# Attention stage: the eight gathers of a group's expert rows issued in one run, behind the LayerNorm root and the bias addition

## The reference, cut to what matters

```python
x = x + L0_xattn(layernorm(x), ctx, ctx)      # mLSTM cell, 8 heads
x = x + L0_ffn(layernorm(x))                  # mixture of 8 experts, top 2, and one shared expert
x = x + L1_xattn(layernorm(x), ctx, ctx)      # softmax attention, 16 heads
x = x + L1_ffn(layernorm(x))                  # 8 experts by position
```

```python
q = split(layernorm(x) @ Wq.T + bq);  k = split(ctx @ Wk.T + bk);  v = split(ctx @ Wv.T + bv)
x = x + softmax(q k^T * SCALE) v @ Wp.T + bp
```

## Time and profile before

| | us |
|---|---|
| median of 3 timed runs (1168.09 to 1171.35) | 1169.76 |
| the profiled execution, whole | 1156.03 |
| its span in the trace | 1154.0 |

### The profile page before, as it was taken

The page is one execution under the profiler, slowest core; times in us unless marked ns, Lnnn a source line. Parts: engine busy times, 40 slices in busy tenths (PEclk is TensorE's granted clock), DMA queues, the critical chain, the costliest instruction groups (busy, mean ns, idle before and its releaser), DMA issues. The chain is left out here.

```text
span 1154.0 us, 24802 instructions
## 1 busy us (share of the span) xinstructions
PE 957.6 (83%) x9121; PEld 684.5 (59%) x9121; DVE 734.0 (64%) x2271; ACT 534.4 (46%) x848; POOL 507.2 (44%) x566
## 2 busy tenths in 40 slices
PE   6819998665777766999997279899899899989998
PEld 1217776444555543666665157777777778856665
DVE  7776999765566652878776455555566656345553
ACT  2457886422333322676665234445455455323231
POOL 4302675676566660555554765434544521011110
PEclk9959998886778767999999569988989989989999
DMA  8554553321222234233332211111111310024331
GB/s 258 196 156 137 160 164 108 122 95 51 60 60 67 63 99 126 96 126 120 120 125 80 62 36 39 39 29 29 47 38 32 88 43 20 21 69 109 95 92 36
DMA packets 84598, 101.28 MB, mean 88 GB/s; under 512 B 36128, under 2 KB 57312, under 8 KB 83712
## 3 DMA queue, kind: packets, MB, share of 16 engines
q1 hardware_dynamic: 56576, 78.20, 22.2%
q0 software_dynamic: 8192, 16.79, 5.0%
q10 hardware_dynamic: 19712, 4.72, 2.5%
HBM read 64.81 MB, written 30.67 MB: 83 GB/s over the span
## 5 line engine op out<-in xcount | busy, mean ns | idle before, releaser
L1701 ACT ACTIVATE split_table<-attn_psT 128x1024 f32<-128x1024 f32 x64 | 65.5, 1024 | 163.9 <-DMA early_ctxT<-in_ctxT 94.1
L1022 POOL TENSOR_TENSOR moe_h_lo<-moe_hid,moe_h_hi 128x512 f16<-128x512 f32 x78 | 90.6, 1163 | 103.3 <-ACT moe_h_hi L1175 98.4
L1169 ACT ACTIVATE moe_act_g<-moe_psG,split_unscale 128x512 f32<-128x512 f32 x110 | 75.5, 687 | 66.5 <-PE moe_psU L1104 32.4
L1279 DVE SCALAR_TENSOR_TENSOR moe_hid<-moe_psU,split_to_hidden,moe_act_g 128x512 f32<-128x512 f32 x110 | 81.0, 748 | 37.8 <-ACT moe_act_g L1169 37.7
L1592 PE MATMUL attn_psO<-heads_vheads,split_table 128*64 128x18 f32 x2048 | 81.8, 214 | 24.9 <-issue 24.8
L1592 PEld LDWEIGHTS attn_psO<-heads_vheads,split_table 128*64 128x64 f32 x2048 | 72.7, 140 | 37.0 <-issue 35.7
L1764 DVE TENSOR_REDUCE split_table<-attn_psN 128x16 f32<-128x1024 f32 x62 | 75.7, 1221 | 17.0 <-PE attn_psN L1555 9.0
L1175 ACT ACTIVATE moe_h_hi<-moe_hid 128x512 f16<-128x512 f32 x110 | 68.4, 622 | 35.0 <-DVE moe_hid L1279 17.6
L1016 POOL DMA_INDIRECT scratch_xs<-cell_xn,res_row x64 | 63.1, 986 | 41.5 <-DVE res_row L1273 24.3
L1788 DVE RECIPROCAL split_table<-attn_psO 128x16 f32<-128x16 f32 x64 | 16.5, 257 | 101.8 <-PE attn_psO L1592 66.1
L1016 POOL DMA_INDIRECT scratch_xs<-moe_xn,res_row x64 | 63.2, 987 | 38.3 <-DVE res_row L1273 20.8
(11 more groups left out here) (282 smaller groups left out, 2788.7 us busy)
## 6 DMA issues: line engine op xcount, KB each, us to landing
early_ctxT<-in_keys SPq DMA_DIRECT2D x16, 512.0 KB, 3.6
scratch_ys<-cell_h SPq DMA_DIRECT2D x26, 256.0 KB, 2.0
early_ctxT<-in_values SPq DMA_DIRECT2D x8, 544.0 KB, 3.7
mlstm_vals<-in_values SPq DMA_DIRECT2D x8, 544.0 KB, 4.0
res_x<-in_x SPq DMA_DIRECT2D x16, 256.0 KB, 6.2
early_ctxT<-in_ctxT SPq DMA_DIRECT2D x16, 256.0 KB, 6.3
attn_in_ctxT<-attn_in_ctxT ACTq DMA_DIRECT2D x64, 64.0 KB
scratch_x<-split_table SPq DMA_DIRECT2D x16, 256.0 KB
```

The source lines that it names most:

```text
L1022: pool.tensor_tensor(h_lo[u % 3][c][:, :], hid[u % 2][c][:, :], h_hi[u % 3][c][:, :], ALU.subtract).then_inc(lo_done[c], 1)
L1169: act.activation(act_g[c][:, :], psG[c][:, :], ACT.Silu, scale=sw.unscale[:, 0:1]).then_inc(silu_done, 1)
L1279: v.scalar_tensor_tensor(out=hid[u % 2][c][:, :], in0=psU[c][:, :], scalar=sw.to_hidden[:, 0:1], in1=act_g[c][:, :], op0=ALU.mult, op1=ALU ...
L1701: act.activation(probT[i % 2][:, :, :, :, :].rearrange("p r b m q -> p (r b m q)"), psT[:, :], ACT.Exp).then_inc(prob_done, 1)
```

## The change

```diff
             add_bias(0)
             add_bias(1)
             for g in range(GROUPS - 2):
-                if there(g + 4):
-                    gather(g + 4, (0, 1))
                 if there(g + 3):
                     ln.root(pool, g + 3, (g + 3) % 2)
+                add_bias(g + 2)
                 if there(g + 4):
-                    gather(g + 4, (2, 3))
-                add_bias(g + 2)
+                    gather(g + 4)
             ffn.ln.power_const(pool)
             ffn.ln.root(pool, 0, 0)
```

## The result

The change makes the kernel slower: median 1221.32 us (1217.76 to 1221.72, 6 runs) against 1169.18 (1155.19 to 1173.89, 6 runs) in the same comparison, a ratio of 1.0489 with a 95% interval of 1.0440 to 1.0537. I had said 1171, and 1158 to 1183. The profiled execution took 1220.95 us, against 1156.03 before. In after, lines from 1527 on are two lower than in the kernel before (values are L1590, combine is L1741); the kernels of the experiments shift them further by what their edits add. The one trace of before is of an execution 13.1 us under its median, the one of after of an execution at its median, so of the 64.9 us between their spans the medians bear out 52.1.

A forecast was written before the change was run, and what follows sets the result against it. It took TensorE to bound the passes, with GpSimd mattering through what it makes others wait for. All terms were 0 except +0.90 us in the last pass, giving 1156.9 profiled, 1171 with 13.7 added for the median; range 1158 to 1183.

The forecast's parts named there:

- GpSimd's own times: In a steady pass, counted from S (the root's start): bias at 1.35, first transfer at 2.84, eighth at 11.73 us.
- Root and bias: On GpSimd in each pass: root still waits for statistics, bias moves 5.1 us ahead with nobody delayed; 0 each.
- The case that the prediction priced at 1.1 us: In a pass, split_peak's second half on VectorE waits for the early bias; covered by VectorE's idle time, so 0.
- Transfers and the new loop: Root, bias, eight transfers, landing, combine, statistics, root: at most 20.42 us, under 20.71; 0 in the ten middle passes.
- the new loop binds: Rival, chance 0.12: transfers in a run of eight land 1 us later, so combine delays passes; 1175 us.
- Last pass: The last pass with gathers, 19.81 us before, takes as long as the pass of 20.71: +0.90 us.
- TensorE in the ten middle passes: Between first and last pass: as many transfers in the same 11 us, so 0; ends -13.6 and +16.5 us.
- The first pass: Loses four transfers ahead of its root, keeps eight behind, taken as one run already before: 0, ends 0 and -1.8 us.
- a longer run holds TensorE up more: Rival, chance 0.20: TensorE's backlog gets no pause, its clock drops more often; about 1187 us, 1179 with half the passes.
- One interruption less: Rival, chance 0.28: TensorE is held up at a run's start, not by each transfer; 1.10 us less a pass, about 1160.

The follow-up runs named there:

- e2: Changed kernel with the bias put behind the unbroken run of eight transfers: 1215.06 us, ratio 1.0423 to the kernel before.
- h1: Changed kernel with an addition of 0.83 us on GpSimd behind each of the first three pairs of transfers: 1161.32 us, ratio 1.0092 to before.
- e4: Changed kernel with transfers issued two at a time, the bias or a wait for ScalarE's exponentials between: 1102.10 us, ratio 0.9435 to before.
- g1: Changed kernel with each indirect transfer fetching 32 rows and not 128, still in runs of eight: 1233.23 us, ratio 1.0573 to before.
- e1: Changed kernel with the bias moved between two runs of four transfers, all behind the root: 1173.53 us, ratio 1.0044 to before.
- e3: Changed kernel without the 96 transfers of groups 4 to 15, whose combines take old rows without waiting: 1095.59 us, ratio 0.9373 to before.
- f2: Changed kernel with the same bytes fetched by SyncE as plain transfers of consecutive rows, in runs of eight: 1095.00 us, ratio 0.9356 to before.
- f5: Changed kernel with GpSimd issuing the 96 transfers as plain ones of consecutive rows, in runs of eight: 1094.88 us, ratio 0.9355 to before.

## Why the prediction was wrong

*GpSimd's own times* were right to 0.01 us: bias at S + 1.35, first transfer at S + 2.84, last one at S + 11.74 (S + 11.73 was said).

*Root and bias* at 0 were right: the root still waits for the statistics (idle for 14.6 us ahead of it), and e2 shows that the bias's place is worth little. The case that the prediction priced at 1.1 us, split_peak behind a bias that came first, did not arise: its second half starts at S + 1.31 (882.26), 0.04 us ahead of the bias, and takes 0.23 us beside 0.22 before.

*Transfers and the new loop* did not bind, as forecast: in after combine comes 4.2 us behind the earliest point that the loop allowed (S + 18.46 against S + 14.26). Its price was sound, though: h1 has 2.51 us of landing where 2.53 was taken. The rival "the new loop binds" (0.12) is false for after, and true for h1.

*Last pass*: +0.90 said; it took 27.96 us (990.32 to 1018.28) where 19.81 had been, +8.2. It was priced at a pass with two runs of four, while it is one with a run of eight.

*TensorE in the ten middle passes* is the step that failed. It took 0, with ends of -13.6 and +16.5; the ten cost 51.0 (718.68 to 990.32 is 271.64, less 220.67). The first pass, at 0 too, adds 5.5 (26.53 less 21.03) and the last 8.2: 64.6 in all, rounding aside. Three things were wrong in it:
- "In the same 11 us as many transfers are made, beside the same values" took the cost to go by the number of transfers. It goes by how many stand in a row: e4 makes the same eight for 0.3 us, g1 fetches a quarter of the rows for 11.
- The upper end came from the longest pass that the trace had, 23.72. But every pass of before had runs of four, so none of them bounds a run of eight. The first pass was even read as "one run of eight, as in effect before"; two runs of four with 1.4 us between are not that, as e1 shows (1.0044 against 1.0489).
- The waits of TensorE were taken as the size of the hold. Gaps on "issue" grow from 23.7 to 27.5 us while 48 us are lost, and in e2 they are 42.9 us for nearly the same loss. How late a result was taken up follows the run better: at most 0.68 us for values with no transfers (e3), 1.51 with four, and now 7.1 with eight. It has to be looked for at every consumer, though: in e2 it is the exponential that is 7.7 us late.

The rival *a longer run holds TensorE up more* (0.20) named the mechanism, and the clock with it, and what I put against it ("the total of transfers is unchanged") was the false step. Its price of 1187 at most was too small by 34 us. *One interruption less* (0.28) has the sign wrong: the hold does not come at a run's start, since pairs cost almost nothing.

The Trainium skill says in "SBUF — State Buffer", "SBUF: two separate sides", that DMA and the compute engines can't slow each other. For plain transfers this case agrees (f2 16.82 and f5 16.69 us a pass, 16.81 with none). For runs of indirect ones a pass of 27.2 us speaks against drawing that conclusion for every transfer, and the measurement decides. It does not show that SBUF is where they meet.

## What to carry to other kernels

If TensorE has work beside them, issue indirect transfers from GpSimd in pairs with 1.6 us or more of other work, or a wait, between (1.1 us took most of the hold away in h1); here that alone took the kernel from 1169.64 to 1102.10 us. When a change makes a repeated thing longer, and not more frequent, the trace of before bounds nothing beyond the length it has: widen the range on that side, or extrapolate from the shortest lengths that it does have. Measure an engine's lateness at those who take its results up, at all of them, and not by its own recorded gaps alone.

## What was not expected of the hardware

- Indirect transfers hold TensorE up from about the third in a row until some 1.6 to 1.8 us past the last one; plain ones through the same queue, with the same bytes (16.79 MB) and the same 8192 packets, do not lengthen a pass at all.
- Size is no lever: 64-byte rows give 27.2 us a pass, as do 512-byte ones, and 32 rows for each transfer 28.1.
- An indirect transfer occupies GpSimd for 0.95 us with 128 rows and for 0.87 with 32, a plain one for 0.54.
- With runs of eight TensorE works at 1.2 GHz for half of the twelve passes, with runs of four in before for a fifth, and with pairs or threes almost never (mean clock 0.99 from 692 to 959 us in both), so the short hold of a third transfer leaves the clock up. In h1 the clock is 0.92 there, with next to no gaps on "issue" but with TensorE waiting for the loop.
- What the two share inside the chip stays open. Only the indirect transfers did it, and bytes, the number of rows, the queue and a busy GpSimd are excluded; how GpSimd makes the descriptors, and how TensorE is fed, could not be looked at separately, and indirect transfers of consecutive rows were not tried. Nor was it tried whether one indirect transfer of more rows, in place of two, would be cheaper.
